# Gathering normalised source rows for the later edge groups, and rectifying the update of the earlier ones in transposed form

## The reference

```python
h = relu(layernorm(x))                                   # every node
em = relu(LN(concat(h[src], h[dst]) @ msg_w + msg_b) * msg_g + msg_beta) * edge_weight
messages = segment_mean(em, dst)                         # 0 for nodes without an edge
y = LN(concat(h, messages) @ upd_w + upd_b) * upd_g + upd_beta
g = sigmoid(h @ gate_w + gate_b)
out = x + g * relu(y) + (1 - g) * h
```

## Time and profile before

| | |
|---|---|
| median of 3 runs | 885.0 us (884.76 to 885.63) |
| the profiled execution's own time | 884.2 us |
| its span, first to last instruction | 882.5 us |
| DVE busy | 839.0 us (95%) |
| ACT busy | 827.3 us (94%) |
| PE busy | 671.8 us (76%), weight loads 524.5 us |
| POOL busy | 621.3 us (70%) |
| DMA moved | 107.96 MB, mean 122 GB/s |

### The profile page before, as it was taken

One profiled execution on the slowest core, in us unless ns is written; L12 is line 12 of the kernel. 1 busy time (PEld: TensorE's weight loads), 2 busy tenths in 40 slices (PEclk: granted clock), 3 DMA queues, 4 the chain that ended last, 5 costly groups with the idle time before them and its releaser, 6 DMA issues.

```text
span 882.5 us, 20426 instructions
## 1 busy us (share of the span) xinstructions
PE 671.8 (76%) x4448; PEld 524.5 (59%) x4448; DVE 839.0 (95%) x3820; ACT 827.3 (94%) x3476; POOL 621.3 (70%) x602
## 2 busy tenths in 40 slices
PE   1888888888788888876677878787887877777871
PEld 1655555555555555554566767676666766666760
DVE  6899999999999999999988999999999999999893
ACT  2899999999999999998899999999999999999972
POOL 4777777777777777777577777666666657655377
PEclk9999999999999999998789899889899899998985
DMA  5355665666565566653132232332212111211110
GB/s 154 93 175 183 179 180 178 179 196 196 182 205 190 195 200 188 197 190 116 57 106 80 73 108 85 102 96 93 70 58 70 58 66 59 69 63 48 55 66 33
DMA packets 60437, 107.96 MB, mean 122 GB/s; under 512 B 14567, under 2 KB 16439, under 8 KB 60371
## 3 DMA queue, kind: packets, MB, share of 16 engines
q1 hardware_dynamic: 39756, 71.88, 24.4%
q0 software_dynamic: 18912, 34.84, 13.9%
q10 hardware_dynamic: 1702, 0.53, 0.3%
HBM read 56.01 MB, written 55.12 MB: 126 GB/s over the span
## 4 chain that ended last, share of the span: by engine, by line
ACT 78%; issue 9%; DVE 5%; POOL 3%; PE 2%; ACTq 1%; DMA 1%; POOLq 0%
ACT hrow L395 22%; ACT junk L402 21%; ACT work L1070 8%; ACT xload L395 7%; ACT work L433 6%; ACT lnv L377 4%; POOL out L607 3%; ACT at L1070 2%; ACT work L1127 2%; ACT work L1125 2%; ACT rs L382 1%; ACT work L1075 1%; DVE st L353 1%; DMA shift_col<-in_L_gnn_upd_beta 1%; ACTq L113 1%
## 5 line engine op out<-in xcount | busy, mean ns | idle before, releaser
L607 POOL DMA_INDIRECT out<-work,sidx x196 | 202.5, 1033 | 122.5 <-issue 56.5
L602 POOL DMA_INDIRECT ring<-in_x,src_i x196 | 210.2, 1072 | 72.1 <-issue 57.6
L395 ACT ACTIVATE hrow<-xload,nb,rs 128x128 f32<-128x128 f32 x392 | 208.4, 980 | 1.3 <-DVE nb L388 1.3
L402 ACT ACTIVATE junk<-py 128x128 bf16<-128x128 f32 x588 | 198.3, 589 | 4.4 <-PE py L1246 3.6
L402 ACT ACTIVATION_READ_ACCUMULATOR junk<-py 128x1 f32 x588 | 184.9, 523 | 0.0
L602 POOL DMA_INDIRECT ring<-in_x,gidx x140 | 148.5, 1061 | 46.1 <-issue 41.7
L1075 ACT ACTIVATE work<-pa,shift_col,gain_col 128x512 f32<-128x512 f32 x94 | 119.2, 1268 | 0.0
L1246 PE MATMUL py<-w_u,work 128*128 128x129 f32 x784 | 116.4, 293 | 0.0
L1204 PE MATMUL pt<-ident,hrow 128*128 128x128 f32 x588 | 102.5, 300 | 10.5 <-ACT hrow L395 10.2
L1246 PEld LDWEIGHTS py<-w_u,work 128*128 128x128 f32 x784 | 97.3, 195 | 21.8 <-issue 21.8
L1070 ACT ACTIVATE work<-pt 128x512 f32<-128x512 f32 (+1 forms) x99 | 106.5, 1076 | 3.0 <-PE pt L1204 3.0
(11 more groups left out here) (170 smaller groups left out, 1956.4 us busy)
## 6 DMA issues: line engine op xcount, KB each, us to landing
xload<-in_x SPq DMA_DIRECT2D x98, 256.0 KB, 3.4
out<-work SPq DMA_DIRECT2D x98, 256.0 KB
running_sums<-acc SPq DMA_DIRECT2D x49, 256.0 KB, 2.1
staged_target_rows<-work SPq DMA_DIRECT2D x14, 256.0 KB, 3.2
ring<-staged_target_rows SPq DMA_DIRECT2D x14, 256.0 KB, 3.2
ring<-in_x,src_i POOLq DMA_INDIRECT x196
out<-work,sidx POOLq DMA_INDIRECT x196, 2.2
ring<-in_x,gidx POOLq DMA_INDIRECT x140, 3.0
```

Source lines behind the costliest of these rows:

```text
L395: last = nc.scalar.activation(dest[:, m, :], rows[:, m, :], ACT.Relu, bias=nb[:, s4, at + m:at + m + 1], scale=rs[:, s4, at + m:at + m + 1])
L402: last = nc.scalar.activation(junk[:, j, k, :], prod[:, k, 0:H], ACT.Square, scale=scale, accum_out=mv[:, slot, at + k, 1:2])
L602: pool.indirect_dma_start(out=dest, out_offset=None, in_=rows, in_offset=bass.IndirectOffsetOnAxis(ap=idx, axis=0), **(if_tail if rows is ...
L607: pool.indirect_dma_start(out=out, out_offset=bass.IndirectOffsetOnAxis(ap=idx, axis=0), in_=rows, in_offset=None, **if_tail).then_inc(s, 16)
```

## The change

Two changes, and what they need:

- `TURNED_EDGES = 29`: the update of edge groups 0 to 28 is rectified as in the node stage: `scaled` on DVE, a flip into `pa` on PE (`turned`), one relu on ACT, a flip back into `pa` on PE (`back`), and `gated_sum` on DVE in place of `final`. `pa` is also the target of `aflip`, which now waits for the gated sum of three groups before.
- `LATE = 29`: the node stage also stores its normalised rows `hrow` to DRAM (`h_dram`, 98 stores on SP), and the source rows of edge groups 29 to 48 are gathered from there. For them DVE takes no source statistics and ACT no source rows; PE flips the gathered rows as they are. The gathers of groups 29 to 38 (`UPFRONT = 10`, 40 of them) stand at the start of the edge stage, after all of these stores have landed; those of 29 to 31 are gone from the node stage.
- ACT waits, before it overwrites an `hrow` buffer, for the store of it. ACT's squares of the update now stand ahead of the copy of `pa`. The small bias transfer stands earlier on SP.

```diff
+TURNED_EDGES = 29
-AHEAD = 7
+LATE = 29
+UPFRONT = 10
...
+        h_dram = nc.dram_tensor("normalised_rows", (N, H), f32).ap()
...
+        s_hst = sem4("normalised_rows_stored")
...
+        def late(g):
+
+            return g.at >= LATE
+
...
+        def turned_edges(g):
+
+            return g.at < TURNED_EDGES
+
...
+        def scaled(dve, d, g, slot, at):
+
+            one_mark(d["gamma"], dve, g, nc.vector.tensor_tensor(
+                t_buf[:, g.at % 4], py[:, g.at % 2, :, 0:H],
+                rs[:, slot, at:at + G].unsqueeze(2).to_broadcast([P, G, H]), ALU.mult))
+
+        def gated_sum(dve, d, f, prod):
+
+            d["mix"].after(dve, f)
+            d["back"].after(dve, f)
+            for k in range(G):
+                last = nc.vector.scalar_tensor_tensor(o[:, f.at % 4, k, :], prod[:, k, :], gt[:, f.at % 4, k:k + 1],
+                                                      o[:, f.at % 4, k, :], ALU.mult, ALU.add)
+            one_mark(d["final"], dve, f, last)
 
...
+                q = s.back(4)
+                if live(q, NG):
+                    nd["h"].after(sp, q)
+                    if q.turn is None and q.at == NG - 1:
+                        sp.wait_ge(s_hst[(q.at - 1) % 4], q.back(1).rounds(16, 16))
+                    sp.dma_start(rows(h_dram, q), hrow[:, q.at % 4]).then_inc(s_hst[q.at % 4], 16)
...
             for g in range(1, XS):
+                if g == 4:
+                    sp.wait_ge(s_bsplit, 1)
+                    sp.dma_start(bias3[:, :], bias_b[0:1, :, :]).then_inc(s_b3, 16)
                 node_step(Group(g))
-            sp.wait_ge(s_bsplit, 1)
-            sp.dma_start(bias3[:, :], bias_b[0:1, :, :]).then_inc(s_b3, 16)
...
-                gather(slot(Group(g), 0)[:, k, :], x, src_i[:, c:c + 1], s_gsrc[g % 4])
+                gather(slot(Group(g), 0)[:, k, :], h_dram if g >= LATE else x, src_i[:, c:c + 1], s_gsrc[g % 4])
...
-                        for part in ((gather_dst,) if g < EARLY else (gather_src, gather_dst)) for k in range(G)]
+                        for part in ((gather_src, gather_dst) if EARLY <= g < LATE else (gather_dst,)) for k in range(G)]
...
-            for g in range(AHEAD):
-                ed["h"].after(pool, Group(g), 1)
+            for i in range(4):
+                pool.wait_ge(s_hst[i], 16 * len(range(i, NG, 4)))
+            for g in range(LATE, LATE + UPFRONT):
+                if g >= RING:
+                    ed["h"].after(pool, Group(g - RING), 1)
                 for k in range(G):
-                    gather_src(g + RING, k)
+                    gather_src(g, k)
             refills = [(part, g, k) for g in range(RING, EG)
-                       for part in (((gather_src,) if g >= RING + AHEAD else ()) + ((gather_dst,) if g < DIRECT else ()))
+                       for part in (((gather_src,) if g >= LATE + UPFRONT else ()) + ((gather_dst,) if g < DIRECT else ()))
                        for k in range(G)]
...
                 f = s.back(8)
-                if live(f, EG):
+                if live(f, EG) and not turned_edges(f):
                     final(dve, nc.vector, ed, f, o[:, f.at % 4])
                 if drained and s.at <= EG + 2:
                     early = mix_early(early + 1)
                 if new:
-                    dve.wait_ge(s_gsrc[s.at % 4], s.rounds(G * 16, G * 16))
                     L = ed["stats"]
-                    row_stats(L, s, slot(s, 0), 0)
+                    if not late(s):
+                        dve.wait_ge(s_gsrc[s.at % 4], s.rounds(G * 16, G * 16))
+                        row_stats(L, s, slot(s, 0), 0)
+                if live(f, EG) and turned_edges(f):
+                    gated_sum(dve, ed, f, rows4(pa[:, :]))
                 if live(s.back(1), EG):
-                    minus_mean(dve, ed, s.back(1), 2 * G, -0.5)
+                    minus_mean(dve, ed, s.back(1), 2 * G, -0.5, G if late(s.back(1)) else 0)
                 q = s.back(3)
                 if live(q, EG):
                     if beyond(q, 4):
...
                     node_rows(node)
                 if fin:
                     ed["rstd"].after(dve, s)
-                    one_mark(ed["gamma"], dve, g, by_std(t_buf[:, g.at % 4], py[:, g.at % 2], s.at % 4, 3 * G, g_upd))
-                    beta(dve, ed, g, t_buf[:, g.at % 4], be_upd)
+                    if turned_edges(g):
+                        scaled(dve, ed, g, s.at % 4, 3 * G)
+                    else:
+                        one_mark(ed["gamma"], dve, g, by_std(t_buf[:, g.at % 4], py[:, g.at % 2], s.at % 4, 3 * G, g_upd))
+                        beta(dve, ed, g, t_buf[:, g.at % 4], be_upd)
                 if new:
                     L.begin(dve, s)
                     if s.at >= DIRECT:
...
+                    if beyond(g, 4):
+                        act.wait_ge(s_hst[g.at % 4], g.rounds(16))
...
-                logs(act, ed, s, 4 * G, 1.0 / H)
-                rstds(act, ed, s, 4 * G)
+                a = G if late(s.back(1)) else 0
+                logs(act, ed, s, 4 * G, 1.0 / H, a)
+                rstds(act, ed, s, 4 * G, a)
...
+                if live(s.back(6), EG):
+                    post(act, ed, s.back(6), (s.at + 1) % 4, 3 * G, G, 1.0)
                 g = s.back(5)
                 if live(g, EG):
                     evacuate(ed, g, at_[:, g.at % 2, :], pa[:, :], ACT.Copy, "at", "aflip")
-                if live(s.back(6), EG):
-                    post(act, ed, s.back(6), (s.at + 1) % 4, 3 * G, G, 1.0)
                 g = s.back(1)
                 if live(g, EG):
                     ed["nb"].after(act, g)
                     H_ = ed["h"]
                     H_.begin(act, g)
-                    H_.mark(h_rows(g, hrow[:, (g.at + NG) % 4], slot(g, 0), 0))
+                    if late(g):
+                        H_.mark(h_rows(g, h_dst[:, (g.at + NG) % XS, 0:2], slot(g, 1)[:, 0:2], G))
+                    else:
+                        if g.at < 4:
+                            act.wait_ge(s_hst[(g.at + NG) % 4], 16 * len(range((g.at + NG) % 4, NG, 4)))
+                        H_.mark(h_rows(g, hrow[:, (g.at + NG) % 4], slot(g, 0), 0))
                 if node is not None:
                     node_h(node)
                 if live(s.back(6), EG):
                     gates(act, s.back(6), 0)
                 if live(g, EG):
-                    H_.mark(h_rows(g, h_dst[:, (g.at + NG) % XS], slot(g, 1), G))
+                    a = 2 if late(g) else 0
+                    H_.mark(h_rows(g, h_dst[:, (g.at + NG) % XS, a:G], slot(g, 1)[:, a:G], G + a))
                 if node is not None:
                     node_post(node)
                 if live(s.back(6), EG):
                     gates(act, s.back(6), 1)
                 if live(s.back(7), EG):
-                    ed["gate"].after(act, s.back(7))
-                    gated_relu(act, ed, s.back(7))
+                    if turned_edges(s.back(7)):
+                        turned_relu(ed, s.back(7), pa[:, :])
+                    else:
+                        ed["gate"].after(act, s.back(7))
+                        gated_relu(act, ed, s.back(7))
...
                 g = s.back(5)
                 if live(g, EG):
                     ed["sum"].after(pe, g)
+                    if beyond(g, 3) and turned_edges(g.back(3)):
+                        ed["final"].after(pe, g.back(3))
                     one_mark(ed["aflip"], pe, g, flip(pa[:, :], acc[:, g.at % 4]))
                 g = s.back(2)
                 if live(g, EG):
...
                         last = nc.tensor.matmul(pm[:, k, :], ht_dst[:, (g.at + NG) % 4, k * H:(k + 1) * H], w_all[:, 1, :],
                                                 start=False, stop=k == G - 1)
                     one_mark(ed["msg"], pe, g, last)
+                g = s.back(7)
+                if live(g, EG) and turned_edges(g):
+                    ed["gamma"].after(pe, g)
+                    if live(s.back(5), EG):
+                        ed["at"].after(pe, s.back(5))
+                    elif beyond(g, 1):
+                        ed["final"].after(pe, g.back(1))
+                    one_mark(ed["turned"], pe, g, flip(pa[:, :], t_buf[:, g.at % 4]))
                 g = s.back(1)
                 if live(g, EG):
-                    ed["h"].after(pe, g, 1)
-                    one_mark(ed["flip"], pe, g, flip(pt[:, 0, :], hrow[:, (g.at + NG) % 4]))
+                    if late(g):
+                        pe.wait_ge(s_gsrc[g.at % 4], g.rounds(G * 16, G * 16))
+                        one_mark(ed["flip"], pe, g, flip(pt[:, 0, :], slot(g, 0)))
+                    else:
+                        ed["h"].after(pe, g, 1)
+                        one_mark(ed["flip"], pe, g, flip(pt[:, 0, :], hrow[:, (g.at + NG) % 4]))
                 g = s.back(5)
                 if live(g, EG):
                     if beyond(g, 2):
...
                     ed["flip"].begin(pe, g)
                     ed["flip"].n = 1
```

(48 more changed lines are left out.)

22 lines of the change are left out of this document (11 added, 11 removed).

## The result

The changed kernel takes 911.94 us (median; 910.50 to 915.58), the kernel before 885.32 us (884.76 to 887.11): 1.0303 times as long, 95% interval 1.027 to 1.0337. The forecast was 878.2 us with a range of 866 to 895, a gain where the change is a loss. The profiled execution spans 908.7 us, 26.2 more than the 882.5 of before.

What follows compares the result with a forecast made beforehand. DVE and ACT were taken as near their limit in both stages, PE as having slack. Turned steps +7.8, late steps -13.1 and step 49 -1.5 gave -6.8 us on 884.2, 877.4; plus 0.8 to the median: 878.2 us, range 866 to 895.

Steps and rivals of the forecast that it cites:

- The clock: Turned edge steps: PE never idles longer than about 1.2 us, so its clock was taken as full.
- Rival A: Message matmuls, steps 7 to 36: one in two at half clock, 1.58 us each, +23 us, about 901 us; chance 0.12.
- The loop: Steps 7 to 36: a round through PE and DVE bounds the step at 8.90 us, not 8.63: +7.8 us.
- B: Turned steps: no loop, the busiest engine alone bounds the step at 8.2 us; about 851 us; chance 0.04.
- C: Edge stage: the loop is shorter (8.7) or late steps follow ACT (7.09); about 866 us; chance 0.12.
- The late steps: Edge steps 36 to 49: DVE bounds them at 7.62 us instead of 8.63, -13.1 us.
- Node stage and POOL: Added stores in the node stage, and gathers and scatters on POOL: hidden, each costed at 0.
- D: Late edge steps: POOL's work holds output buffers back, halving the gain; no difference, 883.3 to 886.7 us; chance 0.08.
- E: Node stage: DMA load delays stores or ACT's extra wait costs, +9 us: 887 to 890 us; chance 0.08.
- Rival F: Added transposes in the turned steps run slow whatever the clock, +26 us: about 904 us; chance 0.02.
- The sum: Whole kernel: +7.8 - 13.1 - 1.5 = -6.8 us, giving a forecast of 878.2 us.

Runs made afterwards that it cites:

- e3: Changed kernel plus four unread f32 128x128 matmuls on PE ahead of the running sum's flip in each turned step: 873.44 us, 0.986 of before.
- e4: Changed kernel plus eight unread transposes on PE ahead of the running sum's flip in each turned step: 874.48 us, 0.9867 of before.
- e2: Changed kernel with turned groups only, without late gathers and stores of normalised rows: 926.88 us, 1.0465 of before.
- e13: e4 with four unread transposes instead of eight, on a sound chip: 885.51 us, 1.0019 of before.
- e14: e4 plus one DVE copy per turned step directly behind the gated sum, inside the loop: 884.58 us.
- e15: e4 plus the same DVE copy per turned step ahead of the gated sum, where DVE waits for PE: 875.43 us.
- e1: Changed kernel with late gathers only, no turned groups (TURNED_EDGES = 0): 860.63 us, 0.9708 of before.
- e11: e4 with the gated sum moved on DVE behind the message scaling: 1070.69 us on a chip where the kernel before took 1035.01.

## Why the prediction was wrong

- **The clock (the step that failed).** "I take the clock as full there", because PE never idles longer than about 1.2 us. PE's waits were sized nearly right (1.38 and 0.48 us with four transposes of 0.63 us between, where the forecast had 2.43 us in all), but the conclusion from them was wrong: in 22 of 29 messages, some or all of the work ran at half clock. What I argued from, that a shorter idle stretch than today's 2.07 us keeps the clock, had no row behind it; the trace of before has 13 slow messages among those 29, with waits of 2.07 and 0.38 us in a step, and the changed kernel has 22 with two shorter waits. e3 and e4 remove exactly this and nothing else, and give back 37 to 38 us. The Trainium skill describes this kind of loss ("TensorE: Matmul & The Clock Gate", A second HAM failure mode: psum-queue depth-cycling): PE idles briefly and often between groups of matmuls, and the clock goes to and fro. The trace agrees, with waits of 1.38 and 0.48 us in every turned step.
- **Rival A was right in kind, its count too low.** The place (message matmuls of steps 7 to 36) and the price (1.58 us each, measured 10.47 - 8.90 = 1.57) were right; one in two was expected, three in four came: (22 - 14.5) x 1.58 = 12 us, where A's 901 lies 11 us under the 911.9. The point from which A decides was 4.3 of 29. Its chance of 0.12 was far too low for a mechanism that the earlier trace rows already showed at work.
- **The loop.** 8.90 us forecast; 8.89 to 8.91 measured in the steps at full clock, in after, e2, e3, e4 and e13, but for the first step of each (9.06 to 9.31), which I did not explain. e14 and e15 show that it is this loop. Right, and B (no loop) and the 8.7 of C are refuted.
- **The late steps.** 7.62 forecast, 7.44 measured in most of them, DVE busy 49.79 of 50 us and ACT 46.71: DVE bounds them, as forecast, not ACT. What goes between `final` and nb is 0.99 us (1.62 before, 0.63 after; forecast 1.01). Most of the missing 0.18 us lies in the small moment operations, which I called "only narrower" and costed at nothing. DVE of before, and then of after:

```profile
609.14 0.23 DVE L367 TENSOR_TENSOR mv<-st 128x8 f32<-128x8 f32 x1
609.29 0.16 DVE L368 TENSOR_TENSOR s_dif<-st 128x8 f32<-128x8 f32 x1
609.37 0.16 DVE L369 TENSOR_TENSOR s_var<-st 128x8 f32<-128x8 f32 x1
609.46 0.34 DVE L963 SCALAR_TENSOR_TENSOR acc<-acc,cont_wb 128x128 f32<-128x128 f32 x1
```

```profile
801.46 0.16 DVE L377 TENSOR_TENSOR mv<-st 128x4 f32<-128x4 f32 x1
801.53 0.16 DVE L378 TENSOR_TENSOR s_dif<-st 128x4 f32<-128x4 f32 x1
801.61 0.16 DVE L379 TENSOR_TENSOR s_var<-st 128x4 f32<-128x4 f32 x1
801.68 0.35 DVE L1002 SCALAR_TENSOR_TENSOR acc<-acc,cont_wb 128x128 f32<-128x128 f32 x1
...
803.50 0.68 DVE L509 TENSOR_TENSOR work<-work 128x512 f32<-128x512 f32 x1
804.13 0.16 DVE L398 SCALAR_TENSOR_TENSOR nb<-mv,rs 128x4 f32<-128x4 f32 x1
```

  Three of them take 0.32 us of the queue before and 0.22 after; a fourth, `s_dif` from itself, takes 0.14 and 0.07. The last two rows are `final` and nb of a late step.
- **Node stage and POOL, costed at 0.** The first message of the turned stretch comes 0.9 us earlier than before, not later, with the DMA share at 0.79 (forecast 0.83); e1 with the same stores is 25 us faster. The first scatter starts at 494.64 us (forecast 496), and no turned step but the first is longer than one of the two lengths, so no scatter held DVE there. D had scatters halve the gain of the late steps: they gained 14.5 us, where 13.1 were forecast. Rivals D and E are refuted.
- **Rival F (transposes slow whatever the clock).** Refuted by 0.60 us for four transposes at 604.05 and 604.49. The Trainium skill says in the same page, Part 4: PE-mode transpose, that the full clock doesn't engage for transposes, which don't count as PE-busy in the same way; by that rule e4 would have stayed near 912 us. It took 874.48 with a clock of 1.00, so the measurement speaks against it here.
- **The sum.** With 22 slow messages in it, the prediction's own sum is 878.2 + 22 x 1.58 = 913.0 us; measured 911.94. That these agree to about 1 us is in part luck: the start and the end are 0.9 us shorter each and the late steps 1.4, while the turned stretch and the step from M47 to M48 are 0.7 longer each.

The fastest kernel that was run is e1, late gathers without turned groups: 860.63 us, 0.9708 of before. Since a turned step is 8.90 us at best and an unturned one 8.64, no number of turned groups helps this order of work.

## What to carry to other kernels

When a change turns slack on PE into a loop through PE, price the loop twice, at the full and at the half clock, and give the slow case the weight that the trace already shows: a slow stretch that costs nothing today, because slack hides it, becomes part of the step when the slack goes. That DVE was busy a quarter less and ACT a sixth less said nothing about the step here, since the new dependence ran through all three engines. And the cheapest test of a clock loss is to add useless work in the wait: if the kernel gets faster, the clock was the cause.

## What the runs showed of the hardware

- Eight f32 transposes of 128x128 in each turned step held PE's clock at 1.00 as four f32 matmuls did (874.48 and 873.44 us; 1.09 us for the eight).
- The slow messages are not spread evenly. In the changed kernel five come in a row, then one at full clock, over and over (PE clock in the first 2 us of each message from M15 on: 0.78, 0.70, 0.63, 0.56, 0.50, 1.00, 0.78, ...). Each slow message costs nearly the same, 1.56 to 1.65 us, whichever of these values its first 2 us show.
- In e1, with 8.64 us steps, about every second message also has the clock at 0.50 in it, and the steps keep their length: there the slack of PE hides it, as in before.
- The same kernel can take much longer on another chip: before took 884.9 to 885.8 us on some, 1035 and 1055 us on two others, where the kernels that were profiled have waits of up to 21 us on ACT (e11, ended at 613.42 us) for which the profile names no engine. What stalls them, and whether it is the chip or the time of the runs, stays open.
